# Identity matmuls ahead of each attention and of the query selection, and a pair of blocks projected during a gather, in a two-layer decoder on one core

## What is computed

```python
x = x + _L0_attn_ref(_layernorm(x), ...)              # gated recurrence and feed-forward
x = x + _L0_xattn_ref(_layernorm(x), ctx, ctx, ...)   # attention 0: 16 heads of 8, rotary
x = x + _L0_ffn_ref(_layernorm(x), ...)               # 8 routed experts, the best 2 a token, and a shared one
x = x + _L1_attn_ref(_layernorm(x), ...)              # attention 1: causal, and only the 24 best queries a head
x = x + _L1_xattn_ref(ctx, ctx, _layernorm(x), ...)   # attention 2
x = x + _L1_ffn_ref(_layernorm(x), ...)               # 8 experts, one a token, with a capacity
```

## Time and profile before

| | |
|---|---|
| three runs | 1094.67 us median (1091.3 to 1103.55) |
| the profiled execution | 1101.7 us, span of its instructions 1100.0 us, mean granted clock 0.766 |
| PE busy | 703.9 us (64%) |
| PEld, DVE busy | 451.0 us (41%), 481.0 us (44%) |
| ACT, POOL busy | 312.7 us (28%), 240.3 us (22%) |

### The profile page before, as it was taken

The page is one execution under the profiler, slowest core; times in us unless marked ns, Lnnn a source line. Parts: engine busy times, 40 slices in busy tenths (PEclk is TensorE's granted clock), DMA queues, the critical chain, the costliest instruction groups (busy, mean ns, idle before and its releaser), DMA issues. The chain is left out here.

```text
span 1100.0 us, 19023 instructions
## 1 busy us (share of the span) xinstructions
PE 703.9 (64%) x5168; PEld 451.0 (41%) x5169; DVE 481.0 (44%) x1183; ACT 312.7 (28%) x567; POOL 240.3 (22%) x370
## 2 busy tenths in 40 slices
PE   3434497547998686998044698854899844408860
PEld 2311233225776454655032466521566523305540
DVE  3454323453443442446343555443555343814431
ACT  1124422102445221443012144521244523003330
POOL 4442100040000123522621100013000021051225
PEclk9666698755656668999566799986699965759995
DMA  6589600085330002142148534106544010020002
GB/s 211 153 227 371 148 0 0 6 210 137 91 92 2 0 15 79 39 138 66 40 118 230 132 94 105 32 1 172 141 118 105 30 49 0 1 87 19 24 24 76
DMA packets 108233, 98.57 MB, mean 90 GB/s; under 512 B 9384, under 2 KB 99648, under 8 KB 103936
## 3 DMA queue, kind: packets, MB, share of 16 engines
q1 hardware_dynamic: 101952, 87.87, 29.8%
q0 software_dynamic: 3072, 6.30, 2.0%
q10 hardware_dynamic: 3152, 3.69, 1.0%
HBM read 53.53 MB, written 43.91 MB: 89 GB/s over the span
## 5 line engine op out<-in xcount | busy, mean ns | idle before, releaser
L1128 DVE TENSOR_REDUCE negm<-ps 128x4 f32<-128x512 f32 x192 | 124.6, 687 | 106.2 <-PE ps L1626 105.7
L810 ACT ACTIVATE wa<-ps 128x1024 f32<-128x1024 f32 x96 | 98.3, 1024 | 160.5 <-PE ps L1647 159.0
L1489 PE MATMUL ps<-ident,xn_tm 128*128 128x128 f32 x112 | 30.6, 427 | 149.0 <-DVE xn_tm L977 86.1
L1489 PEld LDWEIGHTS ps<-ident,xn_tm 128*128 128x128 f32 x112 | 19.8, 214 | 159.7 <-issue 143.6
L1626 PE MATMUL ps<-stack 75*128 75x128 bf16 x576 | 66.7, 258 | 10.2 <-DMA stack<-k_scr 8.9
L1663 PE MATMUL ps<-wa,f 128*32 128x128 f32 x1536 | 72.3, 314 | 1.5 <-ACT wa L810 1.0
L1647 PE MATMUL ps<-stack 75*128 75x128 bf16 x576 | 60.5, 244 | 8.3 <-DMA stack<-mT 8.3
L1626 PEld LDWEIGHTS ps<-stack 75*128 75x128 bf16 x576 | 51.3, 116 | 32.6 <-issue 18.1
L1647 PEld LDWEIGHTS ps<-stack 75*128 75x128 bf16 x576 | 49.5, 112 | 22.3 <-DMA stack<-mT 6.5
L1825 PE MATMUL ps<-w_gu,nT 128*128 x92 | 52.1, 649 | 3.2 <-issue 2.6
L552 POOL COPY f<-v0x 128x144 f32 x32 | 9.9, 309 | 195.4 <-ACTq L818 194.2
(11 more groups left out here) (330 smaller groups left out, 1476.3 us busy)
## 6 DMA issues: line engine op xcount, KB each, us to landing
k_scr<-parts SPq DMA_DIRECT2D x72, 192.0 KB, 2.8
q_scr<-parts SPq DMA_DIRECT2D x72, 192.0 KB, 2.9
stack<-q_scr SPq DMA_DIRECT2D x18, 600.0 KB, 5.5
stack<-k_scr SPq DMA_DIRECT2D x18, 600.0 KB, 7.5
w_w<-in_w SPq DMA_DIRECT2D x2, 2048.0 KB
wb<-q_scr SPq DMA_DIRECT2D x6, 600.0 KB, 5.6
f<-k_scr SPq DMA_DIRECT2D x6, 600.0 KB, 7.3
x_scr<-sel SPq DMA_DIRECT2D x2, 1472.0 KB, 9.1
```

Of the source, the lines that this page charges most:

```text
L810: link.release(act.activation(wa[:, u % 2, :], BF[u % 2], ACT.Exp, scale=SCALE), hWA.filled, hWA.at(stage, n * 4 + u), hB.freed)
L1128: v.tensor_reduce(negm[:, g4 * 4:g4 * 4 + 4, j], A[u % 2].rearrange("p (h k) -> p h k", h=4), AX.X, ALU.max, negate=True).then_inc(hA.free ...
L1489: last = tr(T[:, j * S:(j + 1) * S], src(j), ident[:, :])
```

## The change

Three things. First, the helper `keep_warm(bank, count)`: matmuls of the bf16 identity with itself, 512 columns each, whose result is overwritten. 16 of them stand ahead of the first scores of each attention, behind the wait for a free bank and ahead of the wait for the loaded operands, and 14 in each pair of "qp1" between the head sums and the transposition of `sel`. Second, the first pair of "qp1" moves: on VectorE ahead of the combines and statistics of the second half, on GpSimd its two `rstd` ahead of the second half's gather (its two splits of keys stay behind the gather). Third, the positions and expert numbers kept in `selT` move, so that the first pair's copy into columns 0 to 127 doesn't meet them.

```diff
-        pos0, pos0_i = r0[:, 80:112], r0[:, 112:144].bitcast(i32)
-        te0, te0_i = r0[:, 144:144 + 2 * NT0], r0[:, 192:192 + 2 * NT0].bitcast(i32)
+        pos0, pos0_i = r0[:, 80:112], r0[:, 128:160].bitcast(i32)
+        te0, te0_i = r0[:, 160:160 + 2 * NT0], r0[:, 208:208 + 2 * NT0].bitcast(i32)
...
             for h in range(2):
+                if h == 1:
+                    for n in range(2):
+                        block_stats("qp1", n)
                 g.wait_ge(slots_stored[h], 16 * PER)
...
-            stats("qp1")
-            split_stage("qp1", 2)
+            for i in range(NPAIR):
+                if i == 1:
+                    for n in range(2, NBLK):
+                        block_stats("qp1", n)
+                for p in range(2):
+                    split(g, chain, "qp1", 1, i * 2 + p, False)
             attention(1)
...
-            for n in range(NBLK):
-                if n >= 2:
+            for n in range(2):
+                statistics(n)
+
+            def second_half():
+
+                for n in range(2, NBLK):
                     for b in range(n * GB, (n + 1) * GB):
                         combine(b)
-                statistics(n)
-            v.sem_inc(moe0_done, 1)
-
-            query_stage(1)
+                    statistics(n)
+                v.sem_inc(moe0_done, 1)
+
+            for i in range(NPAIR):
+                query_pair(1, i)
+                if i == 0:
+                    second_half()
...
+            def keep_warm(bank, count):
+
+                for _ in range(count):
+                    mm(bank, identb[:, :], identb[:, :].unsqueeze(1).broadcast_to([128, 4, S]), start=True, stop=True)
+
...
+                        pe.wait_ge(hT.freed, hT.at(stage, i * 4 + 2))
+                        keep_warm(T, 14)
                         pe.wait_ge(sel_ready, i + 1)
-                        pe.wait_ge(hT.freed, hT.at(stage, i * 4 + 2))
                         tr(T[:, 0:S], sel[:, :], ident[:, :]).then_inc(hT.filled, 1)
...
-                    if u == 0:
-
-                        pe.wait_ge(stack_loaded[s], m * LOAD + (len(range(s, NSTEP, 3)) * a + 1) * LOAD)
                     pe.wait_ge(hA.freed, hA.at(stage, n * 8 + u))
                     bank = A[u % 2]
+                    if isinstance(n, int) and n == 0 and u == 0:
+                        keep_warm(bank, 16)
+                    if u == 0:
+
+                        pe.wait_ge(stack_loaded[s], m * LOAD + (len(range(s, NSTEP, 3)) * a + 1) * LOAD)
```

More of the change, by code:

```diff
@@ L523, in _, with block_stats @@
             g.sem_inc(consts_ready, 1)
+            def block_stats(s, b):
+                g.wait_ge(stats_done, b + (STAT[s] + 1))
+                chain.settle()
+                link(g.tensor_tensor(ps_a[:, :], mv[:, bass.ts(b, GB), 1], eps_tile[:, :], ALU.add))
+                link(g.tensor_tensor(rstd[:, bass.ts(b, GB)], ps_a[:, :], halves[:, 0, 0:GB], ALU.pow))
+                g.sem_inc(rstd_done, 1)
             def stats(s):
                 with chain.loop(NBLK, 2) as b:
[L528 to L532, removed]
+                    block_stats(s, b)
             def split_stage(stage, per, rope=False):
@@ L1086, in query_stage, with query_pair @@
             def query_stage(a):
-                stage = "qp%d" % a
                 with link.loop(NPAIR, (4, 2 * 3 + SELECT_LINKS, 3)[a]) as i:
+                    query_pair(a, i)
+            def query_pair(a, i):
+                    stage = "qp%d" % a
                     for p in range(2):
@@ L1612, in scores @@
                     j, g4 = u // 4, u % 4
+                    pe.wait_ge(hA.freed, hA.at(stage, n * 8 + u))
+                    bank = A[u % 2]
+                    if isinstance(n, int) and n == 0 and u == 0:
+                        keep_warm(bank, 16)
                     if u == 0:
                         pe.wait_ge(stack_loaded[s], m * LOAD + (len(range(s, NSTEP, 3)) * a + 1) * LOAD)
-                    pe.wait_ge(hA.freed, hA.at(stage, n * 8 + u))
-                    bank = A[u % 2]
                     if a == 1:
```

## The result

| | before | changed |
|---|---|---|
| median of the runs | 1097.53 us (20 runs, 1090.24 to 1108.3) | 1088.14 us (20 runs, 1078.24 to 1096.23) |
| ratio, 95% interval | | 0.9916 [0.9893, 0.9939] |
| profiled execution | 1101.7 us | 1086.8 us |
| its mean granted clock | 0.766 | 0.795 |

The changed kernel is 9.2 us faster (1 less 0.9916, times 1097.53), with an interval from 6.7 to 11.7. The profiled executions lie 14.9 us apart (1101.7 less 1086.8). I use the end of the first half's statistics as that event: 522.90 before and 515.99 now.

A forecast was written before the change was run, and what follows sets the result against it. Between expert layer and attention 1, gathers and then pair 0's and pair 1's chains bound the kernel. 11.5 us won less 4.6 lost gives 6.9 faster: 1087.8 us from a median of 1094.67, range 1077 to 1098.

The forecast's parts named there:

- The chain of pair 0 and 1: Between expert layer and attention 1: pair 0 beside the gather and a shorter pair 1 win 11.5 us, between 7.9 and 12.0.
- step 1 of the working: GpSimd makes two `rstd` first, so the second half's gather begins at about 524.6 and ends at 544.5, 1.3 us later.
- step 3: Pair 0, from the end of GpSimd's key split: 3.11 us to the last head sums and 2.07 of matmuls, until 554.0.
- VectorE beside the gathers: Pair 0: VectorE's copying or scaling operations hold up GpSimd's gather issue by 0.5 us, between 0 and 4.1.
- rival 2: Overlap eaten: casts delay the gather 4.1 us, pair 0's matmuls stay low, gathers exceed 1.4 us each; 1094 us, chance 0.20.
- the upper end of 4.1: Most that VectorE could delay the gathers: two normalised blocks of 2.40 us and four casts of 0.43 us.
- The head of attention 1: 16 bare identity matmuls cost 6 us, faster first scores win back 1.4: 4.6 us lost, between 2.0 and 6.9.
- The heads of attention 0 and 2: Identity matmuls fit into waits: nothing lost or won at attention 0; 0 taken at attention 2, up to 2 us won.
- rival 3: Attention 1 starts cold and its clock returns 25 us later: 19 us lost, 12 net, 1107 us; chance 0.10.
- Rival 1 in its large form: Identity matmuls keep the clock up throughout attention 0: 20 us less, 1068 us; chance 0.07.
- one sign of being wrong: The prediction counts as wrong if, among other signs, attention 0 or 1 keeps another clock than before.
- The small form of rival 1: One or two steps of attention 0, or attention 2's head, at the high clock: 5 us, 1083 us; chance 0.18.

The follow-up runs named there:

- no_head1: The changed kernel without the 16 identity matmuls ahead of attention 1; 1084.38 us, ratio 0.9844 to the kernel before.
- before_again: The kernel before, word for word, run once more to see how far attention 0 varies by itself; ratio 0.9995.
- split_inside_no_head1: The changed kernel with GpSimd's first split of keys between the second half's eighth and ninth gathers, without attention 1's 16 identity matmuls; 1077.28 us, ratio 0.9827.
- through0: split_inside_no_head1 plus one identity matmul ahead of each of the eight score groups in each step of attention 0; 1076.44 us, ratio 0.9817.
- split_inside_bare: The changed kernel with GpSimd's first split of keys between the second half's eighth and ninth gathers, without any identity matmul; 1078.77 us, ratio 0.984.

## Why the prediction was right

**The chain of pair 0 and 1.** Forecast 11.5 us earlier, between 7.9 and 12.0. Between the shown profiles it is 13.9 (86.6 less 72.7); the mean of the five kernels without the overlap is 86.0, that of the three with it as in the changed kernel 73.8, so 12.2. Both lie above the upper end. The mechanism held, and four terms of its sum were off, in both directions, so that part of the nearness is luck.

1. The start of the gather (step 1 of the working) was 2.4 us later and not 1.3: ahead of it stand two `rstd` and waits of 0.35 and 0.87 us. That is 1.1 too hopeful.
2. From the split's end to the last head sums (step 3) I took over the 3.11 us of the kernel before. There ScalarE wrote the queries and the keys in this time, behind a release by VectorE. Now the queries were done at 529.02, and it was one activation for the keys and one for |q|, 1.40 us (543.27 to 544.67): 1.7 too careful. Taking over a gap without asking what fills it was the error.
3. The 14 identity matmuls took 3.97 us and not 5 and ended 0.5 us before `sel`; I had them end 1.0 behind it. With VectorE's selection 0.2 us longer than forecast, `selT` was written 35.8 us behind the statistics and not 37.9 (the 0.5 for the disturbed gather in it).
4. The second half took 10.4 us and not 9.7, its first combine 1.25 us alone, and pair 1 took 26.3 and not 27.2.

So `selT` is 2.1 early, the combines lose 0.6 of it again, and pair 1 is 0.9 shorter: together 2.4, the difference between 11.5 and 13.9. Of the 2.4 us that pair 1 was to win by its earlier loads 2.15 came: 4.94 us of wait before the second split of queries where it had been 7.09, forecast 4.68. The reason, loads ahead of the store in SP's queue, fits the other kernels. In the five without the overlap the second split starts 16.6 to 17.0 us behind the first load (584.78 and 601.76 in the kernel before), whenever pair 1 itself began, and the wait lies between 7.09 and 4.90 us. In the seven with the overlap the wait is 4.91 to 4.94.

**VectorE beside the gathers.** I took 0.5 us, between 0 and 4.1. Measured 0.56: 20.39 less the 19.83 of the earlier trace rows. Five issues are clearly longer than their 0.94 us, the first (1.03), beside a normalisation, and the four beside VectorE's two splits (1.08 to 1.11). All 16 take 1.27 us each with their gaps, far from the 1.4 of rival 2. But the upper end of 4.1 was counted too high: the two normalised blocks run from 516.22 to 519.22, nearly all of it ahead of the first gather at 518.81. Beside the gathers ran 0.41 us of them and four casts of 0.43, together 2.1 us. The rule of the Trainium skill, "SBUF — State Buffer", section "Who interferes with whom", has VectorE's 2-port modes block GpSimd and the making of descriptors. By that rule those 2.1 us would have been lost, as an estimate from these rows; the trace shows interference in these rows, but at about a quarter of that size.

**The head of attention 1.** Forecast 4.6 us lost (6 less 1.4). Measured 5.99 more up to the scores and 1.48 less for the eight maxima (596.49 to 602.63, before 7.62): 4.5. no_head1 shows it as 5.0. In no_head1 four groups of scores ran at the low level and the other four at the high one. The forecast ended with these eight groups; the six steps behind them, where part of the cost may come back, are under no_head1.

**The heads of attention 0 and 2.** In attention 0 the matmuls ended at 239.47, 1.5 us before the first scores of the earlier trace rows, and the transfer of `mT` came at 249.61 in a kernel in which everything before it was some 3 us early as well (the loads by 3.06, the transfer by 3.18): neutral, as forecast. In attention 2 nothing was won, also as forecast.

**The sum and the rivals.** 12.2 less 4.5 is 7.7; timed 9.2, from 6.7 to 11.7, forecast 6.9. That the median, 1088.14, lies 0.3 us from the forecast of 1087.8 is luck: the forecast started from 1094.67, the median of three runs, and that of 20 is 1097.53. Rival 2 (the overlap eaten) and rival 3 (attention 1 cold) did not happen: attention 1's next six steps take 75.7 us, before 76.0. Rival 1 in its large form did not either. By the letter one sign of being wrong came, another clock in attention 0 (0.63, where it was 0.59), but before_again has 0.63 in the same window without any change. The small form of rival 1 can't be settled. The profiled executions show attention 0 shorter by some 5 us with the matmuls at its head, in every kernel; the timed runs allow between nothing and about 5 us. And I have no mechanism for it: in the changed kernel the matmuls run at 234 to 240, the clock from 240 to 288 is 0.55 (before 0.54), and only the stretch from 288 to 320 is higher, 0.87 (before 0.61). What ties the one to the other wasn't tried.

**A better version.** split_inside_no_head1 and through0 are faster than both kernels, by 1.7% and 1.8%, 19 and 20 us. They don't differ from each other by more than the intervals, and neither differs so from split_inside_bare (0.984), which has no identity matmul at all and least in it.

## What to carry to other kernels

When a chain is moved beside other work, look for the one step of it whose engine is occupied there: that step's place in the engine's order decides the gain, and putting it in the middle of a long row of issues gave another 7 to 8 us in the traces. Matmuls that only raise the clock are free where the engine waits anyway. Where they stand on the path they cost their length (6.0 us here) less what the work behind them runs faster (1.5 in the first eight groups, on average some 3 up to the seventh transfer); the scores raised the clock by themselves here. And before a gap of the old trace goes into a sum, ask what filled it and whether that is still there.

## What the runs showed of the hardware

TensorE can be busy throughout and keep the low clock. In the kernel before, TensorE was busy for 22.95 of 23 us of attention 0 at 0.50, while 14 or 16 matmuls of 512 columns, one behind the other for 4 to 6.4 us, brought it from the low to the high pitch, and one of them per score group kept it at 0.93 through the same work. The Trainium skill, "TensorE: Matmul & The Clock Gate", section "Loop structure matters more than you think", has back-to-back matmuls stay warm; the first of these rows disagrees, the others agree. The high level was lost again in a wait of 5.18 us, and in no_head1 without a wait: TensorE was busy for 4.00 of 4 us at 0.57.

VectorE and GpSimd slow each other when they run side by side, and unevenly. GpSimd's issue of a gather went from 0.94 to 1.11 us at most beside VectorE's splits. VectorE's own operations suffered more beside GpSimd's split of keys, in pair 1 of the changed kernel:

```profile
572.14 1.46 DVE L357 TENSOR_TENSOR f<-f,parts 128x512 f32<-128x512 f32 x1
...
582.30 0.69 DVE L357 TENSOR_TENSOR f<-f,parts 128x512 f32<-128x512 f32 x1
```

The same subtraction takes 1.46 us while GpSimd subtracts too (571.90 to 573.06) and 0.69 us alone.
